# Expert weights ahead of the gathered rows on SyncE's queue, and scale and shift of the router's rows on VectorE instead of GpSimd

## The chip, the cores and the metric

The kernel runs on one core of a Trainium2 chip. The metric is device time in microseconds, from the first to the last instruction with what the launch adds. The core has TensorE (PE: matmuls and transposes, into the PSUM banks), VectorE (DVE), ScalarE (ACT), GpSimd (POOL) and SyncE (SP), which here only issues DMAs. Each engine runs its own instructions in program order; between engines order exists only through semaphores, on which an instruction waits. What stands behind a waiting instruction in the same queue waits too, also when it has nothing to do with that wait.

## What is computed

Four images of 256 channels x 1024 positions go through a convolutional attention block, a second attention block and a mixture of eight experts. The case is about the last part:

```python
def _L1_ffn_ref(x, gate_w, w1, b1, w2, b2, ln_g, ln_b):
    x_norm = _layernorm(x, ln_g, ln_b)            # ... * g + b
    xf = x_norm.reshape(B * S, D)                 # 4096 tokens x 256
    probs = jax.nn.softmax(xf @ gate_w, axis=-1)
    dispatch_w, expert_idx = jax.lax.top_k(probs, TOP_K)      # 2 of 8 experts
    ...
    for e in range(E):
        h = jax.nn.gelu(xf @ w1[e] + b1[e], approximate=False)   # 256 -> 1024
        y = h @ w2[e] + b2[e]                                    # 1024 -> 256
        out = out + combine[:, e:e + 1] * y
    return x + out.reshape(B, S, D)
```

All is float32. A product is made of three fast passes over a high and a low part of each operand: ScalarE rounds to the high part (`hs[0]`, `w1s[n][0]`), VectorE subtracts to get the low part, and TensorE multiplies high by high, high by low and low by high.

## The kernel before

**Images.** The four images run one after the other. Each has eight query tiles of first attention (softmax tiles), a list `R` of 24 products between the two attentions, and eight tiles of second attention. The router of image b-1 (layernorm, gate, top 2, slots) is spread through the work of image b. Its layernorm is in two halves h of four token tiles: ScalarE's `normal` writes `xf` without scale and shift (semaphore `xf_norm`), GpSimd's `affine` (lines 657 to 664) multiplies `xf` by the row `g_row` and adds `b_row`, each over 128x1024 elements, and signals `xf_ready`. TensorE then transposes `xf` for the gate (`gate_turn`, `turn_q`), and GpSimd's `send_rows` writes each token's row twice, by an indirect DMA, into `sorted_rows`, where rows lie sorted by expert.

**Expert steps.** A step s takes 256 sorted rows of one expert: TensorE turns the rows over (`x_turn`, line 1910), then works in eight pieces f: a first product of six matmuls, three pieces ahead, ScalarE's GELU (line 1016), VectorE's split into `hs` (lines 1608 and 1610), and a second product of six matmuls. VectorE adds the bias of the previous step's result (`y_bias`, line 1554, at f = 1), ScalarE weighs it (`y_scale`, line 1034, at f = 3), GpSimd adds it to `acc_rows` with two indirect DMAs (`scatter`, line 751), waits for their landing, and reads the numbers and weights of the next rows (`note_step`, lines 741 and 742), which signals `noted`.

In this run 36 steps are live. Steps 0 to 9 are written out (`LOOP_AT` = 5 pairs); they use only rows of the first three images, and the last image's router is put between their pieces by tables as `AFFINE_AT` or `TURN_AT`, whose keys are (step, piece). The later steps run in a loop over pairs, which needs the rows of all images.

**Weights.** The steps alternate between two buffers n. Where a step's expert is not the one of two steps before (`fresh`), SyncE loads `w1r` and `w2r`, 1 MB each, for it (lines 513 and 515). While step s-1 computes, ScalarE's `w_piece` (line 955) and VectorE's (line 1512) split the weights of step s in eight pieces, the first directly after the GELU of piece 0. ScalarE runs in order, so a missing weight holds all later GELUs.

**SyncE's order.** For each s it issues: weights s, then the biases of s (lines 525 and 527; they wait for `y_bias` of step s-2), then the rows of step s+2 (`gather`, line 536; it waits for `x_turn` of s and for `noted` of s). So the weights of s+1 stand behind the rows of s+2. After the written-out steps SyncE writes the last image's residual rows (`rows_of`, line 500), nine pads of 272 KB into the gaps of `sorted_rows` (line 583), waits for all of these and for all rows sent, and enters the loop.

Of the kernel before, what the change touches and what calls it, by code (L numbers as in the profile page):

```python
# [50 lines left out]
def hybrid_block_kernel(nc, x, q_w, k_w, v_w, oT, q_b, v_b, out_b, gn, W1, W2T, a_qk, a_vT, Wout,  # L51
# [37 lines left out]
    with ctx:  # L89
# [239 lines left out]
        af_own = signal("af_own")  # L329
# [91 lines left out]
        AFFINE_AT = {0: (0, 1)}  # L421
        TURN_AT = {(1, 4): 0, (1, 7): 1, (2, 2): 2, (2, 5): 3}
        COLUMNS_AT = {(1, 7): 0, (2, 2): 1, (2, 5): 2, (3, 0): 3}
        GATE_TILES_AT = {(3, 0): (0, 1), (3, 1): (2, 3), (3, 2): (4, 5), (3, 3): (6, 7)}
        READ_AT = (3, 5)
        TOPS_AT = {(3, 6): (0, 1, 2), (3, 7): (3, 4, 5), (4, 0): (6, 7)}
        CHOOSE_AT = (4, 1)
        RANKS_AT = (4, 3)
        EXP_AT = (4, 5)
        SLOTS_AT = (4, 6)  # L430
        WEIGH_AT = (4, 7)
        TABLE_AT = {(5, 1): 0, (5, 3): 1, (5, 5): 2}
        ROWS_AT = {5: (0, 1), 6: (2, 3), 7: (4, 5), 8: (6, 7)}
        STREAM_AT = {(5, 1): 0, (5, 5): 1, (6, 1): 2, (6, 5): 3, (7, 1): 4, (7, 5): 5, (8, 1): 6, (8, 5): 7}
# [27 lines left out]
        def _(sp):  # L462
# [79 lines left out]
            def expert_load(s, n, u):  # L542
# [14 lines left out]
                biases(n, e)  # L557
# [9 lines left out]
            def steps(i, first):  # L567
                for n in range(2):
                    s = i * 2 + n
                    if not first:  # L570
                        expert_load(s, n, i)
                    gather(s + 2, n, False)

            for i in range(LOOP_AT):
                steps(i, i == 0)
            rows_of(B - 1)


            sp.wait_ge(tab_b, 1)
            sp.wait_ge(pad_made, 2)  # L580
            for e in range(E + 1):
                at_row = sp.value_load(pad_at[0:1, e:e + 1], min_val=0, max_val=PAD - STEP) if e < E else PAD
                sp.dma_start(sorted_d[bass.ds(at_row, STEP), :].rearrange("(h p) c -> p h c", p=P),
                             pad_row[:, :].unsqueeze(1).to_broadcast((P, SUB, ROW))).then_inc(pad_in, 16)
            sp.wait_ge(pad_in, (E + 1) * 16)
            sp.wait_ge(rows_in, B * NT * 2 * 16)
            with sp.Fori(LOOP_AT, PAIRS) as i:
                with is_live(sp, i):
                    steps(i, False)
# [5 lines left out]
            for n in range(2):  # L595

                sp.wait_ge(g_in[n], at(s_end, 8, 24))
                sp.sem_inc(sp_held, 1)
            sp.wait_ge(tok_out, (B + 1) * 16)
# [12 lines left out]
        def _(pool):  # L612
# [44 lines left out]
            def affine(b, h):  # L657
                c = slice(4 * h, 4 * h + 4)
                pool.wait_ge(xf_norm, at(b, 2, h + 1))
                g.tensor_tensor(xf[:, c, 0:C], xf[:, c, 0:C],  # L660
                                g_row[:, :].unsqueeze(1).to_broadcast((P, 4, C)), ALU.mult).then_inc(af_own, 1)
                pool.wait_ge(af_own, at(b, 2, h + 1))
                g.tensor_tensor(xf[:, c, 0:C], xf[:, c, 0:C],
                                b_row[:, :].unsqueeze(1).to_broadcast((P, 4, C)), ALU.add).then_inc(xf_ready, 4)

# [11 lines left out]
            def image(b, first, last):  # L677
# [3 lines left out]
                for i in range(NT):  # L681
                    first_norm(b, i)
                    if not first and i in (2, 3):
                        affine(b - 1, i - 2)
# [70 lines left out]
            def steps(i):  # L755
                for n in range(2):
# [4 lines left out]
                    if isinstance(i, int):  # L761
                        for h in AFFINE_AT.get(s, ()):
                            affine(B - 1, h)
# [291 lines left out]
        def _(dve):  # L1055
# [100 lines left out]

            def gate_read(b, at_bank=0, c=0):
# [882 lines left out]

R_CONSTANTS = 15

OWN_IMAGE = 115


# [40 lines left out]
```

## Time and profile before

| | us |
|---|---|
| median of three runs | 1393.78 |
| lowest, highest | 1392.93, 1395.61 |
| the profiled execution, its own time | 1394.08 |
| its span in the trace | 1392.4 |
| images, until the experts' first step | about 703 |
| steps 0 to 35 of the experts | about 645 |
| last products, sums and output | about 45 |

The profile gives for each engine its busy time, and a list of instructions with the idle time before each and what ended it. Times in the trace are counted from the start of the span. A step is measured here from the `x_turn` of one step to that of the next: what is called stretch k begins with the `x_turn` of step k, which TensorE does at piece 1 of step k-1, and holds the rest of step k-1 and piece 0 of step k. ScalarE's first piece of weights k falls at the start of stretch k.

### The profile page before, as it was taken

The numbers are of one execution on the slowest core, as the hardware profiler recorded it, in microseconds if no ns is written. First come the engines' busy times: TensorE is split into PE (matmuls) and PEld (weight loads), VectorE is DVE, ScalarE is ACT, GpSimd is POOL, SyncE is SP. The second block draws the span as 40 slices with busy tenths as digits, with TensorE's granted clock in tenths as the row PEclk, the third lists the DMA queues.
The fourth block names the chain that finished last, engine by engine and source line by source line (L and its number), as shares of the span: only waits on it lengthen the run. The fifth ranks groups of instructions, "written<-read, shape, count | busy, mean of one in ns | idle before, by whom it ended". The sixth has DMA issues, their size and how long they took to land. (4 is left out here: it accounts for less than half of the span.)

```text
span 1392.4 us, 24905 instructions
## 1 busy us (share of the span) xinstructions
PE 1176.3 (84%) x8066; PEld 1097.9 (79%) x8067; DVE 805.4 (58%) x1915; ACT 573.0 (41%) x1042; POOL 293.3 (21%) x323
## 2 busy tenths in 40 slices
PE   6999999999999999999976877455776675699993
PEld 5898998889898898989876867455775575599992
DVE  4674566656666566664676556254655465475651
ACT  3432535325353254532445545243434344354431
POOL 2010003005040050400433123321222121133330
PEclk9999999999999999999998998878897887899997
DMA  4000000001000010000425254555345435423337
GB/s 148 1 31 1 1 0 32 31 1 65 3 31 31 1 65 1 31 1 5 149 77 143 40 152 129 162 149 144 98 103 146 144 97 147 138 54 58 58 54 246
DMA packets 82147, 103.35 MB, mean 74 GB/s; under 512 B 11792, under 2 KB 71312, under 8 KB 82064
## 3 DMA queue, kind: packets, MB, share of 16 engines
q1 hardware_dynamic: 68624, 84.96, 19.3%
q0 software_dynamic: 13440, 17.32, 7.1%
q8 instruction: 48, 0.79, 0.2%
q14 instruction: 35, 0.29, 0.1%
HBM read 74.05 MB, written 29.25 MB: 74 GB/s over the span
## 5 line engine op out<-in xcount | busy, mean ns | idle before, releaser
L1645 PE MATMUL ps<-w2s,hs 128*128 128x256 f32 x1728 | 274.2, 298 | 168.7 <-DVE hs L1610 168.4
L1645 PEld LDWEIGHTS ps<-w2s,hs 128*128 128x128 f32 x1728 | 243.6, 206 | 176.1 <-DVE hs L1610 174.7
L1645 PE MATMUL ps<-xt,w1s 128*128 128x256 f32 x1746 | 271.4, 294 | 0.0
L1645 PEld LDWEIGHTS ps<-xt,w1s 128*128 128x128 f32 x1746 | 241.7, 202 | 0.0
L751 POOL DMA_INDIRECT acc_rows<-y_w,now_s x72 | 120.6, 1675 | 361.8 <-ACT y_w L1034 220.7
L1016 ACT ACTIVATE h<-ps,b1t 128x256 f32<-128x256 f32 x288 | 137.1, 478 | 99.0 <-PE ps L1645 79.5
L1512 DVE TENSOR_TENSOR w1s<-w1r,w1s 128x512 fp32r<-128x512 f32 x88 | 60.1, 685 | 184.4 <-ACT w1s L955 184.4
L955 ACT CAST w1s<-w1r 128x512 fp32r<-128x512 f32 x100 | 61.5, 617 | 236.2 <-DMA w1r<-in_w 221.2
L1610 DVE TENSOR_TENSOR hs<-h,hs 128x256 fp32r<-128x256 f32 x288 | 127.7, 444 | 9.9
L1608 DVE CAST hs<-h 128x256 fp32r<-128x256 f32 x288 | 91.2, 317 | 66.4 <-ACT h L1016 38.2
L1645 PE MATMUL ps<-xs,wh 128*128 128x512 f32 x384 | 121.1, 397 | 1.6 <-issue 1.6
L1645 PEld LDWEIGHTS ps<-vk,pr 128*128 128x128 f32 x768 | 95.9, 190 | 4.5 <-DVE pr L1466 2.3
L1645 PE MATMUL ps<-vk,pr 128*128 128x256 f32 x768 | 97.1, 282 | 1.8 <-DVE pr L1466 1.8
L673 POOL DMA_INDIRECT sorted_rows<-xf,slot_i x64 | 69.7, 1090 | 134.0 <-ACT prob L902 100.6
L1645 PE MATMUL ps<-vs,pr 128*128 128x256 f32 x768 | 97.7, 282 | 0.0
L1645 PE MATMUL ps<-xs,qs 128*128 128x512 f32 x384 | 95.3, 397 | 0.0
L1645 PE MATMUL ps<-qs,ks 128*128 128x512 f32 x384 | 92.0, 390 | 0.0
L1645 PEld LDWEIGHTS ps<-vs,pr 128*128 128x128 f32 x768 | 91.9, 188 | 0.0
L1645 PEld LDWEIGHTS ps<-xs,wh 128*128 128x128 f32 x384 | 69.4, 188 | 14.5 <-issue 1.8
L1645 PEld LDWEIGHTS ps<-qs,ks 128*128 128x128 f32 x384 | 70.1, 188 | 13.2
L1645 PEld LDWEIGHTS ps<-xs,qs 128*128 128x128 f32 x384 | 69.8, 188 | 13.4
L1461 DVE TENSOR_REDUCE neg_max<-ps 128x1 f32<-128x1024 f32 x32 | 39.2, 1224 | 68.6 <-PE ps L1645 68.6
(232 smaller groups left out, 1805.0 us busy)
## 6 DMA issues: line engine op xcount, KB each, us to landing
w1r<-in_w SPq DMA_DIRECT2D x22, 1024.0 KB, 5.0
w2r<-in_w SPq DMA_DIRECT2D x22, 1024.0 KB, 7.5
xg<-sorted_rows SPq DMA_DIRECT2D x38, 272.0 KB, 2.8
b2t<-in_b SPq DMA_DIRECT2D x36, 128.0 KB, 3.0
xn<-in_x SPq DMA_DIRECT2D x4, 1024.0 KB, 4.9
acc_rows<-r_out SPq DMA_DIRECT2D x4, 1024.0 KB, 4.9
rows<-acc_rows SPq DMA_DIRECT2D x8, 512.0 KB, 7.3
out_tokens<-cols_out SPq DMA_DIRECT2D x8, 512.0 KB, 8.9
```

What stands on the lines that cost most here:

```text
L673: g.indirect_dma_start(out=sorted_d, out_offset=bass.IndirectOffsetOnAxis(ap=slot_i[:, k, t:t + 1], axis=0), in_=xf[:, t, :], in_offset=No ...
L751: g.indirect_dma_start(out=acc_d, out_offset=bass.IndirectOffsetOnAxis(ap=now_s[:, n, h:h + 1], axis=0), in_=y_w[:, n, h, :], in_offset=No ...
L955: a.copy(hi[:, c], (w1r, w2r)[f // 4][:, n, c]).then_inc(ws_act, 1)
L1016: a.activation(h32[:, gi % 4, :], bank(gi % 4, STEP), ACT.Gelu, bias=b1t[:, n, f:f + 1]).then_inc(h_act, 1)
L1461: v.tensor_reduce(neg_max[:, i:i + 1], bank(2 * (i % 2), count=2), AXX, ALU.max, negate=True).then_inc(s2_max, 1)
L1512: v.tensor_tensor(lo[:, c], (w1r, w2r)[f // 4][:, n, c], hi[:, c].bitcast(F32), ALU.subtract).then_inc(ws_dve, 1)
L1608: v.tensor_copy(hs[0][:, f, :], h32[:, gi % 4, :]).then_inc(h_hi, 1)
L1610: v.tensor_tensor(hs[1][:, f, :], h32[:, gi % 4, :], hs[0][:, f, :].bitcast(F32), ALU.subtract).then_inc(h_lo, 1)
L1645: ins = t.matmul(out, left[l], right[r], start=first and n == 0, stop=last and n == 2, **more)
```

## The change

SyncE's `expert_load` is cut in two. For each s it now issues weights s+1, the rows of s+2, and the biases of s+1. The pads move from behind the written-out steps to behind step 6, and `rows_of` for the last image to behind step 8. `affine` moves from GpSimd to VectorE, in four parts. In the images' bodies these stand behind the normalisation of softmax tiles (loop index 4, 5 and 7) and at the third product of `R`; for the last image at pieces 1, 2, 5 and 6 of step 1. The rest of the last image's routing moves by some pieces, its residual rows (`STREAM_AT`) come eight pieces or more earlier, and the sending of rows is spread anew over steps 5 to 8.

```diff
-        AFFINE_AT = {0: (0, 1)}
-        TURN_AT = {(1, 4): 0, (1, 7): 1, (2, 2): 2, (2, 5): 3}
+        AFFINE_AT = {(1, 1): (0, 0), (1, 2): (0, 1), (1, 5): (1, 0), (1, 6): (1, 1)}
+        TURN_AT = {(1, 5): 0, (2, 0): 1, (2, 3): 2, (2, 6): 3}
...
-        ROWS_AT = {5: (0, 1), 6: (2, 3), 7: (4, 5), 8: (6, 7)}
+        ROWS_AT = {5: (0,), 6: (1, 2, 3), 7: (4, 5), 8: (6, 7)}
...
-            def expert_load(s, n, u):
+            def load_weights(s, n, u):
 
                 sp.wait_ge(ws_act, at(s, 8, -8))
                 sp.sem_inc(sp_held, 1)
                 sp.wait_ge(ws_dve, at(s, 8, -8))
                 sp.sem_inc(sp_held, 1)
-                e = expert(s)
                 with sp.If(sp.value_load(fresh[0:1, bass.ds(s, 1)], min_val=0, max_val=1) == 1):
-                    weights(n, e)
+                    weights(n, expert(s))
                 with sp.Else():
                     no_weights(n, u)
+
+            def load_biases(s, n):
                 sp.wait_ge(h_act, at(s, FC, -FC))
                 sp.sem_inc(sp_held, 1)
                 sp.wait_ge(y_dve, at(s, 1, -1))
                 sp.sem_inc(sp_held, 1)
-                biases(n, e)
+                biases(n, expert(s))
...
-            def steps(i, first):
+            def steps(i):
                 for n in range(2):
                     s = i * 2 + n
-                    if not first:
-                        expert_load(s, n, i)
+                    begin = isinstance(i, int) and s == 0
+                    if not begin:
+                        load_weights(s + 1, 1 - n, (i if n == 0 else i + 1))
                     gather(s + 2, n, False)
+                    if not begin:
+                        load_biases(s + 1, 1 - n)
+                    if isinstance(i, int):
+                        if s == 6:
+                            write_pads()
+                        if s == 8:
+                            rows_of(B - 1)
...
+            def affine(b, h, part):
+
+                c = slice(4 * h, 4 * h + 4)
+                row = ((g_row, b_row)[part])[:, :].unsqueeze(1).to_broadcast((P, 4, C))
+                if part == 0:
+                    dve.wait_ge(xf_norm, at(b, 2, h + 1))
+                    step(v.tensor_tensor(xf[:, c, 0:C], xf[:, c, 0:C], row, ALU.mult))
+                else:
+                    settle()
+                    v.tensor_tensor(xf[:, c, 0:C], xf[:, c, 0:C], row, ALU.add).then_inc(xf_ready, 4)
```

On SyncE, in the body of the loop over pairs, the first step of a pair before. The rows stand last:

```order
L549 TENSOR_LOAD fresh
L549 ISA x2
L549 COMPARE_AND_BRANCH
L513 ISA
L513 DMA w1r<-in_w 128x2x1024
L515 DMA w2r<-in_w 128x8x256
...
L525 ISA [waits y_dve]
L525 DMA b1t<-in_b 128x8
...
L535 ISA [waits noted]
...
L536 DMA xg<-sorted_rows 128x2x272
```

The same place in the changed kernel:

```order
L543 ISA
L547 ISA [waits ws_act,ws_dve]
L547 TENSOR_LOAD fresh
...
L512 DMA w1r<-in_w 128x2x1024
L514 DMA w2r<-in_w 128x8x256
...
L534 ISA [waits noted]
...
L535 DMA xg<-sorted_rows 128x2x272
L539 REGISTER_ALU [waits h_act,y_dve]
...
L524 DMA b1t<-in_b 128x8
```

The weights now follow the biases of the step before with no wait on `noted` between them; that wait stands between the weights of s+1 and the biases of s+1.

On SyncE, behind step 6 of the written-out steps, in the changed kernel (before, the pads stood behind step 9):

```order
L526 DMA b2t<-in_b 128x256
L587 TENSOR_LOAD pad_at [waits pad_made,tab_b]
L587 ISA x2
L588 ISA
L588 DMA sorted_rows<-pad_row 128x2x272
...
L588 DMA sorted_rows<-pad_row 128x2x272 x2
L547 TENSOR_LOAD fresh [waits ws_act,ws_dve]
...
L512 DMA w1r<-in_w 128x2x1024
```

The nine pads now stand between the biases of step 7 and the weights of step 8.

On GpSimd, between step 0 and step 1 of the experts, before. The four rows of `affine` stand ahead of the sums of step 0:

```order
L741 CAST now_s<-xg 128x2
L742 ISA
L742 COPY now_w<-xg 128x2
L660 TENSOR_TENSOR xf<-xf,g_row 128x4x256 [waits xf_norm]
L663 TENSOR_TENSOR xf<-xf,b_row 128x4x256 [waits af_own]
L660 TENSOR_TENSOR xf<-xf,g_row 128x4x256 [waits xf_norm]
L663 TENSOR_TENSOR xf<-xf,b_row 128x4x256 [waits af_own]
L751 DMA acc_rows<-y_w,now_s 4096x256 [waits noted,y_act]
```

On VectorE, in step 1 of the changed kernel, where the first two of them now stand:

```order
L1566 TENSOR_TENSOR y_b<-ps,b2t 128x512 [waits y_mm]
L1524 TENSOR_TENSOR w1s<-w1r,w1s 128x512 [waits ws_act]
L1160 TENSOR_TENSOR xf<-xf,g_row 128x4x256 [waits xf_norm]
L1622 CAST hs<-h 128x256 [waits y_mm,h_act]
L1624 TENSOR_TENSOR hs<-h,hs 128x256 [waits h_hi]
L1557 TENSOR_TENSOR xt<-ps,xt 128x512 [waits xt_hi]
L1163 TENSOR_TENSOR xf<-xf,b_row 128x4x256 [waits own]
L1622 CAST hs<-h 128x256 [waits y_mm,h_act]
```

They are gone from GpSimd's queue, and stand between the splits of `h` and of the weights on VectorE.

## Rows read from the trace of the kernel before

**Rows 1.** The page: busy time by engine, and PE's in 40 slices.

```profile
PE 1176.3 (84%) x8066; PEld 1097.9 (79%) x8067; DVE 805.4 (58%) x1915; ACT 573.0 (41%) x1042; POOL 293.3 (21%) x323
PE   6999999999999999999976877455776675699993
```

**Rows 2.** Who waited for whom: us in total, times, longest us.

```profile
ACT w1s L955 <- DMA w1r<-in_w: 221.2, 20, 27.3
PE ps L1645 <- DVE hs L1610: 168.4, 32, 24.8
```

**Rows 3.** Stretches: start:end, length, busy PE, PEld, DVE, ACT, POOL, clock, DMA share, GB/s.

```profile
944.58:1029.90 85.32, 55.38 (x403) 54.37 (x402) 47.11 (x108) 35.95 (x78) 15.40 (x16) 0.82 0.46 128
1041.52:1231.38 189.86, 123.67 (x903) 121.28 (x901) 104.38 (x238) 79.73 (x173) 34.86 (x36) 0.82 0.45 128
1231.00:1348.00 117.00, 117.00 (x1010) 117.00 (x1008) 70.64 (x183) 49.17 (x110) 36.73 (x40) 1.00 0.34 58
```

**Rows 4.** Timelines of stretches 22 to 24: start, us, engine, instruction, [idle before].

```profile
1167.47 0.39 SPq L536 DMA_DIRECT2D xg<-sorted_rows  x1
1169.63 0.38 SPq L513 DMA_DIRECT2D w1r<-in_w  x1
...
1177.61 0.35 SPq L525 DMA_DIRECT2D b1t<-in_b  x1
1178.14 0.35 SPq L527 DMA_DIRECT2D b2t<-in_b  x1
...
1178.40 0.92 ACT L1034 ACTIVATE y_w<-y_b,now_w 128x256 f32<-128x256 f32 x2
...
1188.13 0.39 SPq L536 DMA_DIRECT2D xg<-sorted_rows  x1
...
1191.46 0.39 SPq L513 DMA_DIRECT2D w1r<-in_w  x1
...
1196.52 0.62 ACT L955 CAST w1s<-w1r 128x512 fp32r<-128x512 f32 x1 [11.09 <-DMA w1r<-in_w]
...
1200.15 0.93 ACT L1034 ACTIVATE y_w<-y_b,now_w 128x256 f32<-128x256 f32 x2
```

**Rows 5.** DMAs issued from 944 to 1231: count, KB each, median us to landing.

```profile
w1r<-in_w SPq DMA_DIRECT2D x13, 1024.0 KB, 5.0
...
acc_rows<-y_w,now_s POOLq DMA_INDIRECT x28, 3.9
```

**Rows 6.** The same for 828 to 839 (first two), and for 560 to 671 (last).

```profile
w1r<-in_w SPq DMA_DIRECT2D x1, 1024.0 KB, 6.7
...
sorted_rows<-xf,slot_i POOLq DMA_INDIRECT x3, 6.5
...
sorted_rows<-xf,slot_i POOLq DMA_INDIRECT x6, 2.7
```

**Rows 7.** Stretches 2 and 3, 6 and 7, 8 and 9, 10 and 11, columns of Rows 3.

```profile
729.31:779.23 49.92, 33.48 (x235) 32.42 (x233) 28.97 (x57) 23.57 (x51) 13.69 (x11) 0.82 0.44 117
809.12:849.18 40.06, 27.88 (x202) 26.57 (x201) 27.39 (x79) 19.26 (x42) 11.96 (x13) 0.87 0.53 146
849.18:885.86 36.68, 26.48 (x202) 25.96 (x201) 18.48 (x44) 19.17 (x42) 14.86 (x15) 0.86 0.48 126
885.86:944.58 58.72, 26.75 (x202) 26.36 (x201) 22.97 (x52) 17.50 (x38) 11.90 (x14) 0.74 0.56 165
```

**Rows 8.** SyncE's pads, from the timeline of 886 to 906.

```profile
888.65 11.45 SPq L583 DMA_DIRECT2D sorted_rows<-pad_row  x9
```

**Rows 9.** Timelines around 740 of POOL, DVE, PE, and 1024 columns on DVE.

```profile
740.00 2.35 POOL L663 TENSOR_TENSOR xf<-xf,b_row 128x1024 f32<-128x1024 f32 x1
...
740.04 2.60 DVE L1610 TENSOR_TENSOR hs<-h,hs 128x256 fp32r<-128x256 f32 x1
...
742.69 1.65 PE L1645 MATMUL ps<-w2s,hs 128*128 128x256 f32 x6 [3.78 <-DVE hs L1610]
...
700.89 1.22 DVE L1466 TENSOR_TENSOR pr<-prob,pr 128x1024 fp32r<-128x1024 f32 x1
```

More of the change, by code:

```diff
@@ L565, in _, with write_pads @@
             biases(1, expert(1))
-            def steps(i, first):
+            def steps(i):
                 for n in range(2):
                     s = i * 2 + n
-                    if not first:
-                        expert_load(s, n, i)
+                    begin = isinstance(i, int) and s == 0
+                    if not begin:
+                        load_weights(s + 1, 1 - n, (i if n == 0 else i + 1))
                     gather(s + 2, n, False)
-            for i in range(LOOP_AT):
[L575 to L584, printed above, removed]
+                    if not begin:
[5 more added lines that the diff above has]
+                            rows_of(B - 1)
+            def write_pads():
+                sp.wait_ge(tab_b, 1)
+                sp.wait_ge(pad_made, 2)
+                for e in range(E + 1):
+                    at_row = sp.value_load(pad_at[0:1, e:e + 1], min_val=0, max_val=PAD - STEP) if e < E else PAD
+                    sp.dma_start(sorted_d[bass.ds(at_row, STEP), :].rearrange("(h p) c -> p h c", p=P),
+                                 pad_row[:, :].unsqueeze(1).to_broadcast((P, SUB, ROW))).then_inc(pad_in, 16)
+            for i in range(LOOP_AT):
+                steps(i)
             sp.wait_ge(pad_in, (E + 1) * 16)
@@ L588, in _ @@
                 with is_live(sp, i):
-                    steps(i, False)
+                    steps(i)
             s_end = final_step(sp)
@@ L598, in _ @@
                 sp.sem_inc(sp_held, 1)
+            sp.wait_ge(b_in[0], at(s_end, 16, 48))
+            sp.sem_inc(sp_held, 1)
             sp.wait_ge(tok_out, (B + 1) * 16)
@@ L655, in tail_scales @@
                 g.tensor_tensor(tl_s[:, c], tl_r[:, 0, c], ones[:, 0:4], ALU.add).then_inc(tl_out, 1)
[L657 to L664, printed above, removed]
             def send_rows(b, tiles):
@@ L682, in image @@
                     first_norm(b, i)
-                    if not first and i in (2, 3):
-                        affine(b - 1, i - 2)
                 if not last:
@@ L1415, in image @@
                         norm1(i - 2)
+                    if not first and i in (4, 5, 7):
+                        affine(b - 1, *((0, 0), (0, 1), None, (1, 0))[i - 4])
                     if i == 6:
@@ L1439, in image @@
                                         (qs, ks)[o][0][:, m, c].bitcast(F32), ALU.subtract).then_inc(r_dve, 1)
+                    if not first and gi == 2:
+                        affine(b - 1, 1, 1)
                     if gi == TN_AT - 1:
@@ L1566, in on @@
                     tail_stats(B - 1, STATS_AT[s, f])
+                if (s, f) in AFFINE_AT:
+                    affine(B - 1, *AFFINE_AT[s, f])
                 if (s, f) == READ_AT:
@@ L2041 @@
 R_CONSTANTS = 15
-OWN_IMAGE = 115
+OWN_IMAGE = 117
 def kernel(**inputs):
```

27 lines of the change are left out of this document (12 added, 15 removed).

## The prediction

> **What bounds the kernel now.** Read the busy line and TensorE's slices first [rows 1]. TensorE is busy for 84% of the span, nearly full through the images (the first half) and again late, and has holes between. So the change can win little in the images and much in the experts' steps. Then read who waited for whom [rows 2]: ScalarE waited 221.2 us in 20 places for `w1r`, and TensorE 168.4 us for VectorE's `hs`, which is the same wait passed on: ScalarE's GELU stands behind the weight cast, VectorE's `hs` behind the GELU. Then the stretches [rows 3]. Ten steps without new weights take 117.0 us, 11.7 each, with TensorE busy throughout at clock 1.00. The 13 loop stretches with new weights (four, then nine) take 85.32 + 189.86 = 275.2 us, 21.2 each, with TensorE busy 13.8 of them at clock 0.82 (between the levels of 1.2 and 2.4 GHz). So each loses 9.5 us to late weights, part of it as slow matmuls after the hole. One timeline shows why they are late [rows 4]: the weights' DMA goes out at 1191.46, 3.3 us behind the rows' DMA of 1188.13, which waited for `noted`, that is for the sums of two steps before to land. Nothing in the weights needs that wait.
>
> **Weights ahead of the rows, in the loop.** The weights of s+1 now follow the biases of s, hence `y_bias` of step s-2, instead of the rows. In the cycle shown the biases went out at 1178.14; add 0.35 for that issue, about 1.8 to reach the weights as between rows and weights (1167.47 + 0.39 to 1169.63), and 1.1 more once per pair at the loop's end (3.33 instead of 2.16). They would go at 1180.3 or 1181.4 instead of 1191.46 and land 5.0 later [rows 4, 5], at about the time when ScalarE began to wait (1196.52 - 11.09 = 1185.4). So the direct wait goes, nearly all of it.
>
> What is late next? Three bounds for such a step. TensorE: 11.7 [rows 3]. VectorE: it was busy (47.11 + 104.38) / 13 = 11.65 per stretch, with the affine not in it [rows 3]; in order and with hardly a gap, so 11.7 to 12. The third is the old chain, which is not cut but halved: `noted` no longer holds the next weights, but it holds the biases behind the rows, and these hold the weights of one step later. Over two steps it runs: end of `y_w` to the rows' DMA 1179.32 to 1188.13, 8.8; rows to weights 2.16 or 3.33, plus what now stands between, two bias issues with their gap (1177.61 to 1178.49, 0.9) and a further register load and branch (estimate 0.9, half of the 1.8 above): 4.0 or 5.1; weights to ScalarE's cast 1191.46 to 1196.52, 5.1; cast to the end of the next `y_w` 1196.52 to 1201.08, 4.6 [rows 4]. Together 22.5 or 23.6 for two steps, 11.8 each. All three bounds fall together, so the price is decided by what makes the chain longer.
>
> That is the DMA engines. The weights used to be alone; now they go out about when GpSimd's sums do. In this trace there is one such meeting [rows 6]: indirect rows sent during a load of weights landed after 6.5 us instead of 2.7, and `w1r` after 6.7 instead of 5.0. Both ends for the chain: nothing, 11.8 per step; or the full +3.8 and +1.7, 29.1 / 2 = 14.5. There four row DMAs met the load, here two sums do, so I take somewhat over half, 2.9: 26.5 / 2 = **13.2 per step**. TensorE then idles 1.6 us a step; stretches 8 and 9 [rows 7] show the clock at 0.86 over a deep hole and a shallow one together, and I take 1.00 for shallow holes alone. Gain 275.2 - 13 x 13.2 = **103.6**.
>
> **The written-out steps.** Stretches 2 and 3 take 49.9 [rows 7]. The weights of 2 go out hardly earlier, since the rows of 2 still stand ahead of them and wait for `noted` of step 0. The weights of 3 go out in time, a wait of about the mean of 221.2 / 20 = 11 goes [rows 2]. TensorE was busy 33.5 in the two, part of it at the slow clock, and VectorE 29.0 plus 4.9 of affine: I take 15 for stretch 3 and 21.2 for stretch 2, together 36.2, gain **13.7**. Stretches 6 and 7 take 40.1 with VectorE busy 27.4, of which the first has the tables: 18.8 (VectorE-bound, slots and weighing moved in) and 12.3, gain **9.0**. Stretches 4 and 5, without new weights, cost the same.
>
> The pads: nine issues took 11.45 us [rows 8]. They now stand between the biases of step 7 and the weights of step 8. Without them those weights would be in time; with them they go out 11.4 later than that, and SyncE has no slack for it. So a hole of about 10 stays in stretch 8, about what the mean hole was: 36.7 for stretches 8 and 9 becomes 20.9 + 11.9, gain **3.9**. Stretch 10 had the worst hole, 27.3 [rows 2], since the weights of 10 stood behind `rows_of`, the pads and the last rows sent. Now they stand behind `rows_of` alone, 1 MB that they share the engines with (about 2.5 us). Weights 11 are the first that wait for the last rows, sent during step 9: some 3.5 late. 58.7 becomes 14.2 + 14.5, gain **30.0**.
>
> **Affine on VectorE.** It adds four instructions of 1.22 (as 1024 columns from SBUF took [rows 9]), 4.9 per image, and removes four of about 2.4 from GpSimd. But GpSimd's held VectorE: while the one of 740.00 ran, a `hs` subtraction of 256 columns took 2.60 us and TensorE stood 3.78 us [rows 9]. So in step 1 the trade is 4.9 of VectorE work for up to four such holds of 2.2; I put it within the 13.7. In the images TensorE is nearly full [rows 1] and VectorE waits for it, so the same trade hides under TensorE: 0, with bounds of -2 and +3 for three images (one product that comes late at the third of `R`). If that cover were gone it would cost 14.6.
>
> The Trainium skill (SBUF — State Buffer, section "SBUF: two separate sides") states that VectorE and GpSimd share a pair of ports as an exclusive lock, held for a whole instruction, and that a VectorE operation with two SBUF inputs takes it too. [...]
>
> **Sum.** 103.6 + 13.7 + 9.0 + 3.9 + 30.0 = 160.2 off the profiled execution's 1394.08, which is 0.3 from the median: **1234**.
>
> **The rivals.** *The engines bound, not the DMAs.* If the sums and weights pass each other freely, the 13 steps take 11.8: 18 less, 1216. For it: one meeting in the trace is thin evidence, and the first MB of weights needs 5.0 of some 12 us. Against it: in that meeting the rows landed only about when the weights did. The Trainium skill (DMA: Bandwidth & Descriptors, section "Queues, rings and completion order") has each DMA engine serve its queues in turn, packet by packet, which would let a small sum through before a long load ends and so speaks for this case.
>
> *The chain grows further.* If both the sums and `w1r` are held by the full 3.8, or the holes bring the slow clock back, it is 31.1 / 2 = 15.5 per step: 30 more, 1264. For it: VectorE has no slack left to catch up after a hole, and the 13 stretches ran at a clock of 0.82 [rows 3].
>
> *Slower than before.* One mechanism: the chain over two steps stretched past the old one. The steps now share weights, sums, rows and pads on 16 engines; to eat the 56.6 of the written-out steps as well, a step would have to take 21.2 + 56.6 / 13 = 25.5, thus the chain 51 instead of 23.6, with 27 us of waiting for DMAs that take 5 alone. It would give 1400. Nothing in the rows comes near: the longest landing in them is 6.7.
>
> *The change doesn't do what it says.* If the weights still went out late, for instance since the wait for `y_bias` or SyncE's own loads took as long as `noted`, only stretches 10 and 2 would gain, about 30: 1364. The instructions' order speaks against it.
>
> **How the numbers follow.** Forecast, 12.5 to 14.3 per step and the written-out steps about as summed: 0.56. Engine-bound: 0.22. Longer chain, or half of the written-out gain lost: 0.18. No early weights: 0.02. Slower: 0.02. The range takes in the engine-bound case with another 11 off, and the longer chain with 8 on: 1205 to 1272. About 0.2% is what a measurement of this kernel can tell from no change; faster by more 0.97, within 0.01, slower 0.02.
>
> **What would show it.** In the changed kernel's waits, ScalarE's for `w1r` should fall from 221 to some 45 us, most of it in stretches 2, 8, 10 and 11. The timeline of a loop step should show the weights' DMA before the rows', and the rows' after `noted`. Sums should land after 5 to 7 us instead of 3.9, `w1r` after some 6. If sums still land after 4, the steps are engine-bound at 11.8; VectorE would then be busy for nearly all of a step. If the clock stays under 0.95 in the loop, the holes are deeper than I took. GpSimd should show no `xf<-xf` rows, and VectorE none of 2.6 us. The forecast is wrong if the loop's steps with new weights lie outside 11.6 to 15.5, or if stretch 8 has no hole.

## The result, and the profile after

The changed kernel takes 1252.57 us (median of four runs, 1249.15 to 1255.14), against 1394.69 for the kernel before, measured beside it: ratio 0.898, 95% interval 0.895 to 0.901. So it is faster, by 142 us where 160 were forecast, and 18.6 above the predicted 1234, inside the range. The profiled execution took 1251.13, with a span of 1249.4.

The page of the changed kernel, its busy line and the slices of TensorE with its granted clock, to be held against [rows 1]:

```profile
PE 1150.2 (92%) x8066; PEld 1068.1 (85%) x8067; DVE 815.4 (65%) x1931; ACT 572.1 (46%) x1042; POOL 255.2 (20%) x307
PE   6999999999999999999999879869789888899993
PEclk9999999999999999999999989979899999999996
```

TensorE's busy share rose from 84 to 92%. The images' part (the first 22 or so slices) was full before and is full now. In the experts' part 7s, 8s and one 6 are left: not all holes are gone.

The waits of the changed kernel over the whole span (in total, times, longest), against [rows 2]:

```profile
POOL now_s L740 <- DMA acc_rows<-y_w,now_s: 151.7, 35, 8.1
ACT w1s L952 <- DMA w1r<-in_w: 77.2, 17, 14.3
PE ps L1659 <- DVE hs L1624: 52.8, 33, 10.8
```

ScalarE waited 77.2 us for weights instead of 221.2, in 17 places instead of 20, the longest 14.3 instead of 27.3. The first row has grown: before, GpSimd waited 100.4 us, at most 3.5, for its sums to land; now 151.7 and up to 8.1.

The windows of the changed kernel, by stretches: 2 and 3; 6 and 7; 8 and 9; 10 and 11; the four and the nine loop stretches with new weights; the last row holds the ten without (us, busy time with instructions of each engine, granted clock, DMA share, GB/s). Against [rows 3, 7]:

```profile
729.37:763.71 34.34, 28.69 (x216) 27.78 (x217) 28.84 (x61) 23.61 (x51) 8.49 (x8) 0.85 0.56 163
792.80:822.31 29.51, 24.92 (x202) 23.85 (x201) 27.51 (x82) 16.50 (x36) 9.70 (x9) 1.00 0.63 178
822.31:859.50 37.19, 26.41 (x202) 26.01 (x201) 18.35 (x45) 19.30 (x42) 17.62 (x18) 0.82 0.73 219
859.50:893.56 34.06, 26.50 (x202) 25.18 (x201) 24.37 (x56) 18.99 (x42) 11.36 (x12) 0.90 0.66 196
893.56:950.33 56.77, 49.71 (x402) 48.38 (x401) 45.44 (x106) 33.31 (x73) 16.96 (x18) 0.97 0.58 163
961.94:1088.44 126.50, 111.26 (x902) 107.77 (x901) 103.00 (x236) 77.10 (x170) 34.94 (x38) 0.99 0.62 179
1088.44:1204.72 116.28, 116.28 (x1003) 116.28 (x1001) 70.67 (x183) 49.55 (x110) 36.26 (x40) 1.00 0.33 58
```

Against the forecast, term by term (us; "saved" is the trace before less the trace after):

| stretches | before | after | saved | forecast saved |
|---|---|---|---|---|
| 13 of the loop, new weights | 275.2 (21.17 each) | 183.3 (14.10 each) | 91.9 | 103.6 |
| 2 and 3 | 49.9 | 34.3 | 15.6 | 13.7 |
| 6 and 7 | 40.1 | 29.5 | 10.6 | 9.0 |
| 8 and 9 | 36.7 | 37.2 | -0.5 | 3.9 |
| 10 and 11 | 58.7 | 34.1 | 24.7 | 30.0 |
| 4 and 5 | 29.9 | 29.1 | 0.8 | 0 |
| images, up to stretch 0 | 703.0 | 703.2 | -0.2 | 0 |

These sum to 142.9, the difference of the two profiled executions. Three terms fell short: the loop by 11.7, stretches 10 and 11 by 5.3, and 8 and 9 by 4.4. Three came out above: 2 and 3 by 1.9, 6 and 7 by 1.6, 4 and 5 by 0.8.

How a loop hole arises now is seen in the timeline of the changed kernel, steps around stretch 23 (start, us, engine, line, operation, operands; in brackets the idle time before and what ended it):

```profile
1021.89 0.93 ACT L1031 ACTIVATE y_w<-y_b,now_w 128x256 f32<-128x256 f32 x2
1024.43 0.38 SPq L512 DMA_DIRECT2D w1r<-in_w  x1
1025.73 1.66 POOL L750 DMA_INDIRECT acc_rows<-y_w,now_s  x1 [0.31 <-issue]
1034.46 0.18 POOL L740 CAST now_s<-xg 128x2 int32<-128x2 f32 x1 [7.07 <-DMA acc_rows<-y_w,now_s]
1035.90 0.38 SPq L535 DMA_DIRECT2D xg<-sorted_rows  x1
1037.36 1.66 POOL L750 DMA_INDIRECT acc_rows<-y_w,now_s  x1 [0.30 <-issue]
1037.80 0.34 SPq L526 DMA_DIRECT2D b2t<-in_b  x1
1041.28 0.39 SPq L512 DMA_DIRECT2D w1r<-in_w  x1
1042.76 0.22 POOL L740 CAST now_s<-xg 128x2 int32<-128x2 f32 x1 [3.74 <-DMA acc_rows<-y_w,now_s]
1046.31 0.62 ACT L952 CAST w1s<-w1r 128x512 fp32r<-128x512 f32 x1 [3.78 <-DMA w1r<-in_w]
```

Read it as the chain of the forecast. `y_w` ends at 1022.82, the rows' DMA goes out at 1035.90: 13.1 us where 8.8 were taken. From there the weights follow after 5.4 (5.1 taken), and the cast after 5.0 (5.1 taken). The whole difference lies in the sums. Those issued at 1025.73, 1.3 behind a weights' DMA, are noted 8.7 later; those issued at 1037.36, when the next weights are still 3.9 away, 5.4 later. Before, the sums of 1182.24 were noted at 1186.74, after 4.5:

```profile
1182.24 1.67 POOL L751 DMA_INDIRECT acc_rows<-y_w,now_s  x1 [0.30 <-issue]
1186.74 0.40 POOL L741 CAST now_s<-xg 128x2 int32<-128x2 f32 x1 [2.83 <-DMA acc_rows<-y_w,now_s]
```

Counted from the second of the two sum DMAs, over all sums issued from stretch 12 on in the changed kernel: 3.7 to 4.8 us with no weights under way; 5.1 to 5.5 where weights start 2.3 to 3.9 us behind the sums (four times); 7.3 to 8.9 where they start within 1.3 us of them on either side (eight times).

The mean hides a pattern. At both ends of the loop's part with new weights, late sums make the next weights late; the late weights miss the sums after them, which land early; then the weights are in time again and hit the next sums. So there the holes come in about every second stretch: 12.9 and 16.1 us for stretches 22 and 23, 12.1 and 15.8 for 24 and 25. In between, five sums in a row (955 to 1011) meet a load, noted after 7.3 to 8.2, and the stretches are uneven too: 17.0, 12.6, 14.7 and 13.5 us for 18 to 21.

### The profile page after: what moved, and what is told of

Same layout as the page of the kernel before. It is cut to its first block, busy times and chain, and to the rows that moved or that the text cites. A ratio compares the mean times of both kernels' runs of the same rounds, so it can differ in the third digit from the quotient of the medians.

```text
span 1249.4 us, 24976 instructions
## 1 busy us (share of the span) xinstructions
PE 1150.2 (92%) x8066; PEld 1068.1 (85%) x8067; DVE 815.4 (65%) x1931; ACT 572.1 (46%) x1042; POOL 255.2 (20%) x307
## 3 DMA queue, kind: packets, MB, share of 16 engines
q1 hardware_dynamic: 68912, 85.10, 21.3%
## 4 chain that ended last, share of the span: by engine, by line
PE 67%; DMA 10%; issue 7%; DVE 6%; SPq 4%; ACT 2%; POOL 2%; POOLq 1%; another core or an unknown queue 0%; ACTq 0%; DVEq 0%
PE ps L1659 59%; DMA w1r<-in_w 4%; DMA acc_rows<-y_w,now_s 4%; PE ps L1753 2%; PE ps L1672 1%; SPq L539 1%; PE ps L1701 1%; DVE w1s L1524 1%; DMA rows<-acc_rows 1%; DVE hs L1622 1%; PE ps L1924 1%; DVE hs L1624 1%; PE ps L1762 1%; PE ps L1775 1%; DVE tl_bn L1144 1%
## 5 line engine op out<-in xcount | busy, mean ns | idle before, releaser
L1659 PE MATMUL ps<-w2s,hs 128*128 128x256 f32 x1728 | 258.1, 285 | 53.0 <-DVE hs L1624 52.8
L1659 PEld LDWEIGHTS ps<-w2s,hs 128*128 128x128 f32 x1728 | 227.0, 193 | 61.3 <-DVE hs L1624 50.4
L1659 PE MATMUL ps<-xt,w1s 128*128 128x256 f32 x1746 | 260.4, 286 | 1.0 <-issue 1.0
L1659 PEld LDWEIGHTS ps<-xt,w1s 128*128 128x128 f32 x1746 | 229.3, 192 | 1.8 <-issue 1.6
L1013 ACT ACTIVATE h<-ps,b1t 128x256 f32<-128x256 f32 x288 | 137.5, 478 | 103.6 <-PE ps L1659 60.0
L1624 DVE TENSOR_TENSOR hs<-h,hs 128x256 fp32r<-128x256 f32 x288 | 123.6, 429 | 9.9
L1622 DVE CAST hs<-h 128x256 fp32r<-128x256 f32 x288 | 89.1, 309 | 58.3 <-ACT h L1013 33.9
L952 ACT CAST w1s<-w1r 128x512 fp32r<-128x512 f32 x100 | 61.5, 617 | 77.2 <-DMA w1r<-in_w 77.2
L1659 PEld LDWEIGHTS ps<-vs,pr 128*128 128x128 f32 x768 | 91.9, 188 | 0.5 <-DVE pr L1360 0.5
```

The costliest lines, as they stand in the source:

```text
L952: a.copy(hi[:, c], (w1r, w2r)[f // 4][:, n, c]).then_inc(ws_act, 1)
L1013: a.activation(h32[:, gi % 4, :], bank(gi % 4, STEP), ACT.Gelu, bias=b1t[:, n, f:f + 1]).then_inc(h_act, 1)
L1622: v.tensor_copy(hs[0][:, f, :], h32[:, gi % 4, :]).then_inc(h_hi, 1)
L1624: v.tensor_tensor(hs[1][:, f, :], h32[:, gi % 4, :], hs[0][:, f, :].bitcast(F32), ALU.subtract).then_inc(h_lo, 1)
L1659: ins = t.matmul(out, left[l], right[r], start=first and n == 0, stop=last and n == 2, **more)
```

## The experiments

All variants are of the changed kernel. Stretches in us, from each kernel's trace:

| kernel | median | ratio to before | 2-3 | 8-9 | 10-11 | loop, each |
|---|---|---|---|---|---|---|
| changed | 1252.6 | 0.898 | 34.3 | 37.2 | 34.1 | 14.10 |
| rows first | 1374.2 | 0.985 | 46.9 | 38.9 | 44.9 | 20.58 |
| affine on GpSimd | 1256.9 | 0.901 | 38.0 | 38.2 | 31.4 | 14.08 |
| an eighth of `w2` | 1240.4 | 0.888 | 34.3 | 38.9 | 32.0 | 13.30 |
| an eighth of both | 1213.1 | 0.869 | 31.7 | 33.3 | 25.8 | 12.14 |
| rows issued by GpSimd | 1220.5 | 0.874 | 27.4 | 35.3 | 33.9 | 12.41 |
| pads later | 1249.4 | 0.894 | 34.3 | 32.9 | 33.8 | 14.29 |
| waits behind the weights | 1253.2 | 0.898 | 34.3 | 36.8 | 32.3 | 14.17 |
| weights two ahead | 1208.8 | 0.865 | 26.9 | 30.2 | 31.0 | 12.18 |
| the same, again | 1210.8 | 0.868 | 26.8 | 30.3 | 31.2 | 12.17 |
| two ahead, affine on GpSimd | 1213.9 | 0.871 | 33.3 | 28.0 | 33.6 | 12.21 |
| two ahead, rows on GpSimd | 1221.1 | 0.876 | 27.5 | 34.9 | 30.5 | 12.33 |

The theory, A: the gain is the order of weights and rows; what is missing of it is the sums' leg of the two-step chain, which grows since weights start among the sums. The rivals: the engines set 14.1, the affine or the pads explain the remainder, or the chain is long for another reason.

### The order alone, undone

```diff
-                    if not begin:
-                        load_weights(s + 1, 1 - n, (i if n == 0 else i + 1))
                     gather(s + 2, n, False)
                     if not begin:
+                        load_weights(s + 1, 1 - n, (i if n == 0 else i + 1))
                         load_biases(s + 1, 1 - n)
```

> The changed kernel, with the weights of s+1 again behind the rows of s+2 on SyncE; pads, residual rows and affine stay where the change put them. Theory A (the order of weights and rows is nearly all of the gain): the 13 loop stretches with new weights go back from 14.1 to about 21.2 us, +92, and the written-out ones lose some 35: about 1380 us. Rival (most of the gain comes from the affine on VectorE and from the pads' new place): 1300 or less.

Measured: 1374.15, ratio 0.9845 (0.982 to 0.987). The loop stretches are back at 20.6 and ScalarE waits 199.3 us for `w1r`:

```profile
ACT w1s L951 <- DMA w1r<-in_w: 199.3, 20, 15.0
```

So of the 142 us some 122 are this one exchange of two calls, made on top of the other parts. All other parts together bring 20, of which 13.8 lie in stretches 10 and 11: `rows_of`, the pads and the last rows sent no longer stand in a row ahead of the weights of 10.

### Scale and shift back on GpSimd

```diff
+                        if s == 0:
+                            affine(B - 1, 0)
+                            affine(B - 1, 1)
...
-                if (s, f) in AFFINE_AT:
-                    affine(B - 1, *AFFINE_AT[s, f])
```

The same is done in the images.

> The changed kernel with scale and shift back on GpSimd, for the last image directly after step 0's rows are noted. Theory A: the images don't move (TensorE hides it); in step 1 GpSimd holds VectorE for four times about 2.2 us against 4.9 us of VectorE work saved, and the sums of step 0 go out later: +2 to +6, about 1256 us. Rival (the affine is a large part of the gain): +15 or more, 1268 and above. Second rival (VectorE is the engine that bounds step 1, so taking work from it wins): 1249 or less.

Measured: 1256.9, ratio 0.901 (0.899 to 0.903); the interval overlaps that of the changed kernel. Stretch 2 is 3.6 longer, stretch 11 is 2.2 shorter. The timeline of this kernel shows in step 1 what [rows 9] showed of before:

```profile
724.61 2.35 POOL L671 TENSOR_TENSOR xf<-xf,g_row 128x1024 f32<-128x1024 f32 x1
724.64 2.60 DVE L1633 TENSOR_TENSOR hs<-h,hs 128x256 fp32r<-128x256 f32 x1
```

The subtraction begins 0.03 us behind GpSimd's instruction and ends 0.3 behind it; its mean is 0.43 in the changed kernel's page. In the changed kernel none of VectorE's operations in the experts' part takes over 2 us. So the holds are real, but this pair of runs does not resolve what they cost. It is asked again below, with the holes gone.

### Smaller weights

In the first kernel SyncE loads an eighth of `w2`, in the second an eighth of `w1` and of `w2`.

```diff
-                    weights(n, expert(s))
+                    first_eighth(n, expert(s))
```

> The changed kernel, but each load of new weights after the first two takes all of w1 and only the first eighth of w2 (the rest of the buffer keeps old weights, so the computed values differ; all instructions stay). Theory A (the sums are held while the weights load, and the chain over two steps of sums, rows, biases and weights is longer for it): sums land after about 4 us again, a loop stretch with new weights falls from 14.1 to about 12, 13 x 2.1 = 27 less, about 1223 us. Rival B (VectorE and ScalarE bound the stretch by their work) and rival C (VectorE locks GpSimd out, and so the sums are late): both see the same engine work, no change, 1250 to 1253 us.

> The changed kernel, but each load of new weights after the first two takes an eighth of w1 and an eighth of w2 (the computed values differ; all instructions stay). In the run with w2 alone cut, sums were noted 6.5 to 8.9 us after the second sum's issue wherever a load of w1 began within 1.3 us of it, so one full MB still held them. Theory A (weights under way hold the sums, and with them the chain of two steps): sums noted after about 4.7 as in stretches without new weights, w1 in the buffer about 2 us earlier, loop stretches with new weights at VectorE's 11.7 to 12.0: 13 x 2.2 = 28 less, and 2 us off each remaining hole, about 1220 us. Rival B (work and hand-over of the engines bound the stretch at 13 to 14): 1240 or more.

Measured: 1240.39 (ratio 0.888, 0.885 to 0.891) and 1213.11 (0.869, 0.867 to 0.871). The first gained 12 us, less than half of the 29 that A expected: with `w1`'s 1 MB starting within 1.3 us of the sums they are still noted 6.5 to 8.9 us later. So the second megabyte behind it is not what delays them most. In the second kernel the loop's two parts read, in its windows:

```profile
880.89:930.00 49.11, 47.31 (x402) 46.74 (x401) 45.46 (x105) 33.65 (x73) 15.39 (x16) 1.00 0.34 68
941.65:1050.30 108.65, 105.89 (x902) 104.95 (x901) 101.17 (x233) 77.68 (x168) 34.33 (x36) 1.00 0.32 69
```

157.8 us for 13 stretches, 12.14 each, with TensorE busy 97% at clock 1.00; sums are noted after 3.7 to 5.4 although weights start at the same distance from them. GpSimd's wait for its sums, over the whole span:

```profile
POOL now_s L746 <- DMA acc_rows<-y_w,now_s: 105.1, 35, 3.7
```

With the bytes gone most of the delay is gone: it is traffic, and not that SyncE issues a DMA at that moment. The 12.1 is all but the engines' own need. Even stretches take up to 12.8 and odd ones 11.6 to 12.0, and in stretch 22, one of the long ones, TensorE's only wait is 0.8 us for VectorE's `hs`. It is near the forecast's 11.8 for the engine-bound case, which the changed kernel with its full loads doesn't reach.

Holes stay in stretch 2 (7.9) and 8 (9.3) even with an eighth of the bytes. Those come from the order of the queue, not from traffic.

### The rows on another queue

```diff
+            def gather(s, n, first=False):
+                if not first:
+                    pool.wait_ge(xt_mm, at(s, 1, -1))
+                    ...
+                    pool.wait_ge(noted, at(s, 2, -2))
...
                     load_weights(s + 1, 1 - n, (i if n == 0 else i + 1))
-                    gather(s + 2, n, False)
```

> The changed kernel with the rows' DMAs issued by GpSimd, directly after it noted the rows whose buffer they take, and the wait for pads and for all rows sent moved there too. SyncE issues only weights and biases. Theory A: nothing of the weights waits for the sums any more; loop stretches fall to about 12 (y_bias and VectorE), 27 less, and the hole of 9 in stretch 11 goes: about 1216 us. Rival B (engines bound the stretch): only stretch 11 gains, about 1243. Rival D (GpSimd's time to write the descriptors of 272 KB, on its own queue, puts the sums and notes late enough to hold x_turn): no gain or slower, 1252 and above.

Measured: 1220.51, ratio 0.874 (0.872 to 0.876). This cuts the chain without touching the bytes: SyncE waits for no sums any more. The sums are as late as in the changed kernel, and yet the loop runs at 12.41 and stretch 2 has no hole:

```profile
POOL now_s L735 <- DMA acc_rows<-y_w,now_s: 155.5, 35, 7.9
```

Late sums cost little once no weights stand behind what waits for them. Something is left: from stretch 12 on ScalarE still waits 0.8 to 2.9 us for `w1r` in most of the stretches with new weights, and the total is 4 above the 1216 that A expected. With the kernels of small weights this closes it from both sides: traffic delays the sums, and the queue's order turns that delay into a hole.

### The pads

```diff
-                        if s == 6:
-                            write_pads()
+                        if s == 7:
+                            write_pads(range(7))
                         if s == 8:
+                            write_pads(range(7, E + 1))
                             rows_of(B - 1)
```

> The changed kernel with seven of the nine pads issued behind the biases of step 8 and two behind those of step 9, none ahead of the weights of step 8. Theory A (stretch 8 has its hole of 14.3 us since the nine pads stand ahead of its weights): stretch 8 falls from 25.3 to about 12 and stretch 9 grows by up to 2, -11, about 1241 us. Rival (stretch 8 is late since GpSimd sends six rows' DMAs in step 6 and the notes come late): no change.

Measured: 1249.41, ratio 0.894 (0.892 to 0.896), 3 us where A expected 11, and the interval overlaps that of the changed kernel. SyncE's queue in the changed kernel, where `x9` is one row for nine issues:

```profile
814.24 10.13 SPq L588 DMA_DIRECT2D sorted_rows<-pad_row  x9
826.82 0.39 SPq L512 DMA_DIRECT2D w1r<-in_w  x1
```

SyncE's queue in this kernel, the weights of 8 first, those of 10 last:

```profile
816.41 0.38 SPq L512 DMA_DIRECT2D w1r<-in_w  x1
...
832.27 10.20 SPq L589 DMA_DIRECT2D sorted_rows<-pad_row  x7
845.00 0.40 SPq L535 DMA_DIRECT2D xg<-sorted_rows  x1
...
853.98 0.39 SPq L512 DMA_DIRECT2D w1r<-in_w  x1
```

The weights of 8 now go out 10.4 earlier, and ScalarE's wait of 14.3 for them is gone: 25.3 became 17.6. It did not become the 12 of A: ScalarE's GELU stands still for 6.3 us in that stretch, and the profile names nothing that it waited for. Stretch 9 grew by 3.4 and stretch 10 by 5.1, with a wait of 7.5 for its weights; stretch 11 fell by 5.4 and the loop grew by 2.5. The pads' time on the queue was moved to the next weights, not hidden. So the pads did make the hole in stretch 8, and neither place of the queue that was tried has the slack to take them.

### The waits at the loop's entry

The waits for pads and rows sent, ahead of the loop, were put behind the weights:

```diff
+                    if not isinstance(i, int):
+                        sp.wait_ge(pad_in, (E + 1) * 16)
+                        sp.wait_ge(rows_in, B * NT * 2 * 16)
                     gather(s + 2, n, False)
...
-            sp.wait_ge(pad_in, (E + 1) * 16)
-            sp.wait_ge(rows_in, B * NT * 2 * 16)
```

> The changed kernel with SyncE's wait for the last rows sent and for the pads moved from the loop's entry into the loop, behind the weights and ahead of the rows. Theory A (stretch 11 has a hole of 9 us since the weights of 11 stand behind that wait, which they don't need): stretch 11 falls from 19.6 to 13, about 1246 us. Rival (the hole comes from the biases of 10 behind their rows, thus from the late note): no change, 1252.

Measured: 1253.24, ratio 0.898 (0.897 to 0.900): no change, as the rival had it. SyncE's queue at this place, the changed kernel first:

```profile
864.69 0.36 SPq L535 DMA_DIRECT2D xg<-sorted_rows  x1
866.21 0.72 SPq L524 DMA_DIRECT2D b1t<-in_b  x1
867.67 0.01 SPq L526 DMA_DIRECT2D b2t<-in_b  x1
874.47 0.38 SPq L512 DMA_DIRECT2D w1r<-in_w  x1
```

The same in this kernel:

```profile
865.61 0.29 SPq L535 DMA_DIRECT2D xg<-sorted_rows  x1
...
867.34 0.34 SPq L526 DMA_DIRECT2D b2t<-in_b  x1
873.33 0.68 SPq L512 DMA_DIRECT2D w1r<-in_w  x1
```

The weights of 11 went out 1.1 earlier by the traces' time, and 2.1 earlier if counted from the note ahead of them, which came 0.9 later here. In the changed kernel SyncE did wait at the loop's entry, until 871.6:

```profile
SPq L594 <- DMA sorted_rows<-xf,slot_i: 3.9, 1, 3.9
```

Without that wait its first pass through the loop's own register loads and branches took from 867.7 to 873.3, 5.6 us, where it took 2.9 after the wait and where 1.8 to 3.4 pass between the end of the biases' issue and the weights in later passes of the two kernels. So a first pass was slow with nothing to wait for, and the wait hid part of that; why it is slow was not tried. The larger part of the lateness lies further up: GpSimd waited 8.1 us for its sums and noted at 863.13, and rows, biases and weights follow from there. The step of the forecast that named the last rows' sending had the smaller cause.

### The weights two steps ahead

```diff
-                    if not begin:
-                        load_weights(s + 1, 1 - n, (i if n == 0 else i + 1))
+                    load_weights(s + 2, n, i + 1)
                     gather(s + 2, n, False)
```

The buffers allow it: weights s+2 need only the splitting of weights s to be over, which is so when step s begins.

> The changed kernel with SyncE still issuing everything, but in the round of step s the weights of s+2 instead of s+1, ahead of the rows of s+2. A load then has more than a step until it is needed, and the chain through notes, rows and biases spans three steps for about 28 us. Theory A (only that chain makes the loop stretches 14.1): 11.7 to 12.0 each, 28 less; the holes of stretches 8 (its weights go out ahead of the pads), 10 and 11 go too, another 20: about 1203 us. Rival B (engines bound the loop stretches): loop stays at 14, only stretches 8 and 11 gain, about 1232. Rival E (a load that begins at the end of a step meets the same sums and rows, and x_turn then waits for late rows): above 1225.

Measured: 1208.78, ratio 0.865 (0.863 to 0.867), the fastest of all, and 6 above the 1203 that A expected. The same kernel was taken again beside the two of the next section: 1210.79, ratio 0.868 (0.866 to 0.870).

> The same kernel as the one with the weights two steps ahead (1208.78 us), taken again beside the next two so that they can be compared on one chip. Both theories: 1207 to 1211 us, stretches 2 and 3 together 26.9, the 13 loop stretches with new weights 12.2 each.

No wait of ScalarE for `w1r` is left among the kernel's 60 largest waits. Windows of the second take, stretches 2 and 3, then the loop's two parts:

```profile
729.16:755.92 26.76, 25.89 (x216) 25.31 (x217) 25.96 (x56) 19.28 (x42) 7.94 (x8) 1.00 0.53 131
877.32:926.27 48.95, 48.55 (x403) 48.18 (x402) 45.25 (x105) 33.85 (x74) 15.18 (x16) 0.97 0.62 172
938.64:1047.89 109.25, 105.90 (x903) 104.94 (x901) 102.18 (x235) 76.94 (x169) 36.82 (x36) 1.00 0.65 192
```

The loop moves as many bytes as the changed kernel and runs at 12.17, the same as with an eighth of them. The weights now start mostly 6 to 7 us ahead of the second of the two sum DMAs, and the sums are noted after 3.7 to 5.9. Stretch 2 is without its hole, since its weights no longer stand behind the rows of its own step. In stretches 2 and 3 VectorE is busy 25.96 of 26.76 us: there it is the bound.

What is left lies in stretches 8 to 11, 61.5 us together. The waits of the second take, over the whole span, hold this row:

```profile
ACT h L1012 <- DMA b2t<-in_b: 21.3, 6, 6.1
```

ScalarE's GELU waits for biases now, 12.0 of the 21.3 us in stretches 9 and 10. The biases still stand behind the rows, and those behind the note of sums that land late (GpSimd waited 7.8 us for one of them there). So the fault that the change removed for the weights is left for the biases here.

### Two more steps from there

With no late weights, the two questions left over are asked again: the affine on GpSimd, and the rows issued by GpSimd.

> The weights two steps ahead, with scale and shift of the router's rows back on GpSimd (step 0 for the last image). In the changed kernel this swap was near the noise, since late weights for step 2 hide or follow it. Theory A: with no late weights left, VectorE sets stretch 2, and GpSimd's four instructions hold three of its operations for about 2.2 us more each (6.6) against 3.7 of VectorE's own in stretches 2 and 3, so stretches 2 and 3 together grow from 26.9 to about 30; the images stay as they were; total 3 us more than the run beside it, ratio between the two 1.0025. Rival: TensorE or other work hides the holds, and the two are within 1 us of each other. Other rival: the saved 4.9 us of VectorE work weighs more than the holds, and this one is 1 to 3 us the faster.

> The weights two steps ahead, and the rows' DMAs issued by GpSimd directly after it has read the next numbers, so that biases and weights stand behind no rows. Theory A: with the weights two steps ahead nobody waits for them any more, so taking the rest of the chain away gains nothing: 12.1 to 12.2 per loop stretch, 1207 to 1211 us, as the run beside it. Rival: the biases behind the rows still cost the 12.7 of every second stretch, and it falls to 11.7: 1202 to 1204 us. Other rival: GpSimd's own issuing of rows delays its sums and the last rows' sending, and it is 2 to 5 us slower.

The affine on GpSimd: 1213.86, ratio 0.871 (0.869 to 0.873), 3.1 above the run beside it, though the intervals still touch. The trace is plainer. Stretches 2 and 3 take 6.6 longer. Around their start four of VectorE's operations are held and take 2.4 to 2.9 us each, not three as expected. Two of them, in the timeline of this kernel; the second is the rounding of `h` to its high part `hs[0]`, which VectorE does and not ScalarE (ScalarE rounds only the weights):

```profile
728.44 2.40 POOL L673 TENSOR_TENSOR xf<-xf,b_row 128x1024 f32<-128x1024 f32 x1
728.49 2.89 DVE L1534 TENSOR_TENSOR w1s<-w1r,w1s 128x512 fp32r<-128x512 f32 x1
...
731.31 2.43 DVE L1630 CAST hs<-h 128x256 fp32r<-128x256 f32 x1
```

Its windows for stretches 2 and 3 show the trade, against the first row of the windows above:

```profile
729.44:762.75 33.31, 27.55 (x218) 27.17 (x217) 30.22 (x57) 19.67 (x42) 14.16 (x11) 0.90 0.41 104
```

VectorE is busy 4.3 us longer although the affine is not its own work here (a held operation counts as busy), and the clock fell to 0.90. So 3 to 7 us is what the affine on VectorE is worth once VectorE is the bound there: 3 by the medians, which is close to their noise, and 7 by the stretches.

The rows on GpSimd: 1221.14, ratio 0.876 (0.874 to 0.878), 10 slower where at most 5 were expected. The waits of this kernel from 818 to 885 us (stretches 8 to 11) have at their head:

```profile
PEld ps L1935 <- DMA xg<-sorted_rows: 14.8, 3, 8.5
```

The timeline of its GpSimd there:

```profile
841.96 0.19 POOL L734 CAST now_s<-xg 128x2 int32<-128x2 f32 x1 [6.87 <-issue]
842.99 1.03 POOL L668 DMA_INDIRECT sorted_rows<-xf,slot_i  x1 [0.71 <-issue]
...
848.14 0.78 POOL L745 DMA_DIRECT2D xg<-sorted_rows  x1
```

The rows' DMA stands behind the last image's rows sent on GpSimd's own queue, 6 us after the numbers were read, and TensorE waits for it. That is the same fault as in the kernel before, on another queue. It accounts for 4.6 of the 10 (8 and 9); the loop is 2.1 longer, the images 3.0, which are the same code in both and so within what images vary from take to take (702.1 to 706.1 over all these traces).

## Why the prediction was right, and by how much it missed

**What bounds the kernel: right.** Weights behind rows behind sums. The exchange alone gives 122 of 142 us.

**The loop, 13.2 per step: too short by 0.9.** The mechanism, the chain over two steps, and the side (above the engines' 11.8, below 15.5) were right. Three of its legs fit in the cycle shown: rows to weights 5.4 at the loop's end against 5.1, weights to cast 5.0 against 5.1, `y_w` as taken. The mis-sized term is "somewhat over half" of the DMA contention, 2.9 for both legs. The sums' leg alone took 4.3 more than 8.8, more than the upper bound of 3.8 from [rows 6], and the weights' leg took nothing of its 1.7. (Over the loop that leg took 5.0 to 5.5 seven times and 6.0 to 7.1 five times, where the second sum DMA went out from 2.3 us ahead of the load to 0.1 behind it.) That bound was read from GpSimd's sending of rows, not from its sums. The chain of that cycle is 13.1 + 5.4 + 5.0 + 4.6 = 28.1 against the forecast's 26.5: 0.8 per step, which is most of the 0.9. 13 x 0.9 = 11.7 is the larger half of the 17 missed. That the three bounds fall together at 11.8 holds for the chain of 23.6 alone; 22.5 for two steps would be 11.3 each.

**Engine-bound rival: refuted for this kernel, right for its neighbours.** 12.1 to 12.2 is reached with an eighth of the bytes, or with the same bytes issued elsewhere in the step. The Trainium skill (DMA: Bandwidth & Descriptors, section "Queues, rings and completion order") says that an engine drains one packet and then switches to the next queue with work. By that alone the sums would pass; by the trace they take up to twice as long when the load starts beside them.

**Stretches 2, 3, 6, 7: right** to 1.9 and 1.6 us. Stretch 2 kept its hole (21.5 against 21.2), since the rows of 2 stand ahead of its weights.

**Stretches 8 and 9: the cause right, the hole too small.** A hole "of about 10" was the mean of before; it was 14.3. The weights went out 12.6 after the first pad, 10.1 of it pads. The pads' kernel shows that the cause is the pads.

**Stretches 10 and 11: 28.7 forecast, 34.1 measured.** Stretch 10 was right (14.5 against 14.2). Stretch 11 took 19.6 instead of 14.5: "some 3.5 late" became a wait of 7.6 for the weights of 11, and 1.4 for those of 12 at the stretch's end, since the sums ahead were noted late as well, the same mis-sized leg, and a slow first pass through the loop lay under the wait that was named.

**Affine: right in the images,** as far as it can be seen. There VectorE is busy 11.8 us more and GpSimd 30.1 less up to 703 us, and stretch 0 starts 0.2 later. The instructions took 1.22 us each, as forecast. The forecast counted no gain of its own in step 1; in this kernel what it is can't be told from noise, and it is 3 to 7 us once the holes are gone. Of the "up to four" holds, the trace before has three (2.60, 2.21 and 2.60 us).

**The signs.** `w1r` waits 77 rather than 45; sums noted 7.3 to 8.9 in the bad cycles, later than the 5 to 7 given; the loop's clock 0.97 and 0.99; no `xf<-xf,g_row` on GpSimd; a hole in stretch 8. The larger errors lean one way: the trace before has the engines' traffic well apart, and a single meeting of another kind of transfer set the bound. That the total still came within 18.6 us is in a small part luck: 4.3 us more than forecast in stretches 2 to 7 made up for some of what was missing.

## What to carry to other kernels

On an in-order DMA queue, look at what each issue waits for and who stands behind it: a load that needs nothing must not stand behind a wait. Here ScalarE's waits for weights fell by 144 us and the kernel's time by 142. After moving it, follow the chain again over two steps and look where it lands beside small transfers that someone waits for; when buffers allow it, issue one step earlier, so that neither the wait nor the meeting matters. Then look who still stands behind the wait: here it was the small biases. Work moved within a queue that has no slack (the pads) only moves its hole.

## What the runs showed of the hardware

- GpSimd's sums (256 rows of 1 KB added in DRAM by two indirect DMAs) were noted, in the changed kernel's loop, 3.7 to 4.8 us behind the issue of the second with no load under way, and 7.3 to 8.9 with a load of 2 MB from another queue starting within 1.3 us. In the kernel with the weights two steps ahead a start 6 to 7 us ahead of them delayed them little (3.7 to 5.9), although such a load takes 8.4 us in all. In the kernel with the rows issued by GpSimd, one step ahead, most loads started 2.8 to 5.1 us ahead, and it took 5.6 to 8.4.
- In the changed kernel's loop, seven stretches had waits of ScalarE for weights of 3.3 to 8.4 us: the granted clock was 1.00 in five of them (6.2, 8.4, 4.0, 7.0 and 4.7 us) and 0.89 in two (3.3 and 5.3). TensorE's own longest idle time was 2.2 and 2.6 us in those two, and 3.3, 2.8 and 2.5 us in three of the five, so the length of the gap alone does not sort them. In stretches 2, 8 and 11, with waits of 10.4, 14.3 and 9.0, the clock was 0.76, 0.73 and 0.83. The forecast took 1.00 for shallow holes; the two loop parts had 0.97 and 0.99.
- A GpSimd operation of 1024 columns held not only VectorE's subtractions but also its casts, which have one input: 2.21 us with the affine on GpSimd and 2.43 with the weights two steps ahead as well, where 0.31 is the mean in the changed kernel.
- SyncE's register loads and branches between two DMAs took 5.6 us in the first pass through the loop where no wait stood among them, and 1.8 to 3.4 later.
